# A recommendation tower on one core: group transposes issued two groups of products ahead, and two small layers as three fp32r calls

## The reference

```python
e = jnp.stack([tbl_0[ids[:, 0]], ..., tbl_26[ids[:, 26]]], axis=1)     # (2048, 27, 128)
interactions = jnp.einsum('bfd,bgd->bfg', e, e)
flat_interactions = interactions[:, _TRIU_I, _TRIU_J]                  # 351 a sample
h = jnp.concatenate([e.reshape(B, -1), flat_interactions, dense_ctx], axis=1)
h = jnp.maximum(h @ W_top1 + b_top1, 0.0)      # (3823, 512)
h = jnp.maximum(h @ W_top2 + b_top2, 0.0)      # (512, 256)
y = h @ W_top3                                 # (256, 1)
```

## Time and profile before

| | us |
|---|---|
| median of 3 runs | 712.8 |
| lowest and highest of them | 710.17 and 718.01 |
| the profiled execution | 709.83 |
| its span | 708.0 |
| TensorE busy, share of the span | 574.9, 81% |
| GpSimd busy, share of the span | 416.2, 59% |
| mean granted clock of TensorE | 0.908 |

### The profile page before, as it was taken

One profiled execution on the slowest core, in us unless ns is written; L12 is line 12 of the kernel. 1 busy time (PEld: TensorE's weight loads), 2 busy tenths in 40 slices (PEclk: granted clock), 3 DMA queues, 4 the chain that ended last, 5 costly groups with the idle time before them and its releaser, 6 DMA issues.

```text
span 708.0 us, 7882 instructions
## 1 busy us (share of the span) xinstructions
PE 574.9 (81%) x2578; PEld 504.6 (71%) x2578; DVE 347.6 (49%) x1140; ACT 232.3 (33%) x703; POOL 416.2 (59%) x450
## 2 busy tenths in 40 slices
PE   2606688989889898959959896897968979698898
PEld 1505577868778787948848795786857868697786
DVE  4305462819264563808337281554707355372755
ACT  4204423324251513315232331514315161323441
POOL 6775565666666565665746667365664666556001
PEclk9956899989989998989989899799987999989999
DMA  6613411111111111111111111011110111111000
GB/s 211 217 52 110 131 45 44 46 46 44 45 45 50 41 49 41 48 45 39 47 29 50 44 42 52 27 49 42 46 52 26 49 41 49 42 41 46 12 1 1
DMA packets 19581, 37.84 MB, mean 53 GB/s; under 512 B 7780, under 2 KB 8804, under 8 KB 19540
## 3 DMA queue, kind: packets, MB, share of 16 engines
q0 software_dynamic: 13824, 28.34, 15.1%
q1 hardware_dynamic: 5716, 8.99, 4.0%
HBM read 37.30 MB, written 0.01 MB: 53 GB/s over the span
## 4 chain that ended last, share of the span: by engine, by line
PE 59%; another core or an unknown queue 20%; DVE 8%; issue 6%; ACT 5%; DMA 1%; SPq 0%; ACTq 0%; DVEq 0%
PE ps_acc L298 12%; PE ps_acc L299 11%; PE ps_acc L300 11%; PE ps_gram L323 10%; DVE g_buf L666 6%; PE ps_acc L356 6%; PE ps_t L269 5%; PE ps_gram L400 3%; ACT g_buf L582 2%; DVE emb_x L645 1%; DMA g_buf<-in_W_top 1%; ACT emb_x L534 1%; ACT h_t L571 1%; PE ps_gram L352 1%
## 5 line engine op out<-in xcount | busy, mean ns | idle before, releaser
L242 POOL DMA_INDIRECT emb<-in_tbl,idx x405 | 385.8, 953 | 233.4 <-issue 109.4
L298 PE MATMUL ps_acc<-w_hi,emb_x 128*128 128x512 f32 x432 | 211.1, 489 | 28.7 <-DVE emb_x L645 26.6
L645 DVE TENSOR_TENSOR emb_x<-ps_t,emb_x 128x512 fp32r<-128x512 f32 (+1 forms) x111 | 73.9, 667 | 249.6 <-ACT emb_x L534 165.2
L299 PE MATMUL ps_acc<-w_lo,emb_x 128*128 128x512 f32 x432 | 182.7, 423 | 0.0
L300 PE MATMUL ps_acc<-w_hi,emb_x 128*128 128x512 f32 x432 | 181.0, 419 | 0.0
L666 DVE COPY g_buf<-ps_gram 32x112 f32<-32x112 f32 x480 | 129.8, 270 | 93.6 <-PE ps_gram L323 63.1
L323 PE MATMUL ps_gram<-emb_x 128*128 128x224 f32 x480 | 99.5, 335 | 79.2 <-DVE emb_x L645 41.2
L298 PEld LDWEIGHTS ps_acc<-w_hi,emb_x 128*128 128x128 f32 x432 | 131.9, 305 | 35.3 <-DVE emb_x L645 28.0
L323 PEld LDWEIGHTS ps_gram<-emb_x 128*128 128x128 f32 x480 | 83.4, 231 | 102.0 <-DVE emb_x L645 45.1
L582 ACT ACTIVATE g_buf<-ps_gram 32x112 f32<-32x112 f32 x480 | 122.2, 255 | 99.0 <-PE ps_gram L323 64.8
L534 ACT ACTIVATE emb_x<-ps_t 128x512 fp32r<-128x512 f32 (+1 forms) x111 | 63.1, 583 | 272.7 <-PE ps_t L269 137.4
(11 more groups left out here) (61 smaller groups left out, 163.2 us busy)
## 6 DMA issues: line engine op xcount, KB each, us to landing
g_buf<-in_W_top SPq DMA_DIRECT2D x27, 256.0 KB
emb<-in_tbl,idx POOLq DMA_INDIRECT x405
w_cols<-in_W_top SPq DMA_DIRECT2D x1, 512.0 KB
w<-in_W_top SPq DMA_DIRECT2D x1, 512.0 KB
emb<-in_tbl,idx_first POOLq DMA_INDIRECT x27
w_cols<-in_W_top SPq DMA_DIRECT2D x1, 222.0 KB
idx<-in_ids SPq DMA_DIRECT2D x1, 216.0 KB, 4.9
ctx_rows<-in_dense_ctx SPq DMA_DIRECT2D x4, 32.0 KB
```

The source lines that it names most:

```text
L242: pool.indirect_dma_start(out=emb[:, f * D:(f + 1) * D], out_offset=None, in_=tables[f], in_offset=bass.IndirectOffsetOnAxis(ap=rows, axis ...
L298: pe.matmul(acc, emb_part(0, f), w_hi[:, f, :], start=(f == 0), stop=False)
L299: pe.matmul(acc, emb_part(0, f), w_lo[:, f, :], start=False, stop=False)
L645: dve.tensor_tensor(group_part(1, g), turned_bank(n, g), group_part(0, g).bitcast(fp32), ALU.subtract).then_inc(s_emb_lo, 1)
```

## The change

Three things are changed.

First, the order on TensorE from the second tile on. The turn of a group now stands two groups of features ahead of the features that use it, and the last group is turned before the columns are multiplied. The order of a tile becomes: turn 2, features 0 to 3, turn 3, features 4 to 7, turn 4, features 8 to 11, turn columns, turn 5, features 12 and 13, turn 6, multiply columns, features 14 to 17, turn h1, gram stage with five features in it as before, layer 2, features 23 to 26. ScalarE and VectorE follow: `take_columns` moves behind the split of group 4, and `relu_h1` and `take_h1` behind the split of the last group.

Second, the columns and layer 2 get high and low parts as layer 1 has. Each fp32 call becomes three fp32r calls. ScalarE's copies write the high parts as before; VectorE gets new instructions for the low ones (`split_columns`, two of them a tile, and `split_h1`, one).

Third, the weights of those two layers are split too, in the second tile. They are loaded into places that are free then (the upper part of `g_buf`, `gram`, `h1`), in six transfers where there were four, after all layer-1 weights are split, and cost ScalarE and VectorE five instructions each, once.

The last tile keeps its own order, with the same replacement of calls.

```diff
             def multiply_columns(t):
-                pe.wait_ge(s_cols_out, t + 1)
+                pe.wait_ge(s_cols_hi, t + 1)
                 if t == 0:
-                    pe.wait_ge(s_w_late, 64)
+                    pe.wait_ge(s_late_lo, NCC)
                 for n in range(NCC):
-                    last = multiply_chunk(t, n)
+                    multiply_chunk_hi(t, n)
+                pe.wait_ge(s_cols_lo, t + 1)
+                for n in range(NCC):
+                    last = multiply_chunk_lo(t, n)
                 last.then_inc(s_acc, 1)
...
+            def layer_2(t, acc):
+                pe.wait_ge(s_h1_hi, t + 1)
+                pe.wait_ge(s_h1_lo, t + 1)
+                if t == 0:
+                    pe.wait_ge(s_late_lo, len(LATE))
                 for k in range(K2):
-                    last = pe.matmul(ps_late[:, 0:H2], h1_t[:, k * P:(k + 1) * P], w_2[:, k, :],
-                                     start=(k == 0), stop=(k == K2 - 1))
-                last.then_inc(s_l2, 1)
...
-            BEFORE_UNIT = [2, 0, 0, 2, 0, 0, 1, 0, 0, 1, 0, 0, 1, 0, 0, 0]
-            assert len(BEFORE_UNIT) == UNITS and sum(BEFORE_UNIT) <= NF - 4 * GF
+            BEFORE_UNIT = [0, 0, 0, 2, 0, 0, 1, 0, 0, 1, 0, 0, 1, 0, 0, 0]
...
             for t in range(TILES - 1):
...
+                else:
+
+
+                    turn_group(t, 2)
+                    multiply_next(GF)
+                    turn_group(t, 3)
+                    multiply_next(GF)
+                    turn_group(t, 4)
+                    multiply_next(GF)
                     turn_columns(t - 1)
-                turn_group(t, 4)
-                if t > 0:
+                    turn_group(t, 5)
+                    multiply_next(2)
+                    turn_group(t, 6)
                     multiply_columns(t - 1)
-                multiply_group(t, 3)
-                turn_group(t, 5)
-                if t > 0:
+                    multiply_next(4)
                     turn_h1(t - 1)
...
                 if t > 0:
-                    layer_2(t - 1)
-                while f < NF:
-                    multiply(t, f)
-                    f += 1
+                    layer_2(t - 1, ps_late[:, 0:H2])
+                multiply_next(len(todo))
...
             for t in range(TILES - 1):
                 for g in range(NG):
...
-                    if t > 0 and g == 3:
+                    if t == 1:
+                        for c in LATE_AT[g]:
+                            split_late_weights(c)
+                    if t > 0 and g == 4:
                         take_columns(t - 1)
-                    if t > 0 and g == 4:
+                    if t > 0 and g == 6:
                         relu_h1(t - 1)
-                    if t > 0 and g == 5:
                         take_h1(t - 1)
...
+            def split_columns(t):
+                dve.wait_ge(s_cols_hi, t + 1)
+                dve.tensor_tensor(cols_lo[:, 0:FULL * P], ps_late[:, 0:FULL * P],
+                                  cols_hi[:, 0:FULL * P].bitcast(fp32), ALU.subtract)
...
+            def split_h1(t):
+                dve.wait_ge(s_h1_hi, t + 1)
+                dve.tensor_tensor(h1_lo[:, :], ps_late[:, :], h1_hi[:, :].bitcast(fp32),
+                                  ALU.subtract).then_inc(s_h1_lo, 1)
...
+                        if g == 4:
+                            split_columns(t - 1)
+                        if g == 6:
+                            split_h1(t - 1)
```

More of the change, by code:

```diff
@@ L138, in dlrm_tower_kernel @@
         s_stored = sem("s_stored")
+        LATE = []
+        for n in range(NCC):
+            k = P if n < FULL else REST
+            place = g_buf[0:k, (STAGES - 2 + n) * H1:(STAGES - 1 + n) * H1]
+            LATE.append((place, w_cols_hi[0:k, n, :], w_cols_lo[0:k, n, :]))
+        gram_words = gram[:, :, :].rearrange("p f g -> p (f g)")
+        LATE_AT = [[0, 1, 2], [3], [4], [], [], [], []]
+        for k, place in ((0, gram_words[:, 0:H1]), (2, h1[:, :])):
+            LATE.append((place, w_2_hi[:, k:k + 2, :].rearrange("p k n -> p (k n)"),
+                         w_2_lo[:, k:k + 2, :].rearrange("p k n -> p (k n)")))
         def emb_part(part, f):
@@ L769, in _ @@
             pack_pairs(t, 0, POOL_FROM)
+            for n in range(NCC):
+                split_last_chunk(t, n)
             layer_3(t - 1)
-            take_left_h1(t)
+            split_last_h1(t)
             last_layer_3(t)
```

185 lines of the change are left out of this document (124 added, 61 removed).

## The result

The changed kernel takes 774.9 us (median of 4 runs, 770.9 to 786.3) against 714.1 us for the kernel before beside it. The ratio is 1.083, with a 95% interval from 1.073 to 1.094: slower, where 656 us had been forecast. Its span is 784.2 us, and the mean granted clock fell from 0.908 to 0.869.

What follows compares the result with a forecast made beforehand. It took TensorE to set the pace, waiting on late signals. 14 tiles from 41.2 to 37 us save 58.8 us, once-costs add 2 us: span 651 us; plus 1.8 and 3 us: 656 us, range 610 to 704 us.

Steps and rivals of the forecast that it cites:

- What bounds the kernel: Ahead of the gram stage TensorE idles 6.10 us in the shown tile, mostly for its last turn's late signal.
- The order: Between last turn and gram stage, 5.5 us of work instead of 1.4 us hides 4.3 of 6.5 us lateness.
- fp32 to fp32r: Columns 2.28 to 2.15 us, layer 2 1.54 to 1.45 us; together about 0.2 us a tile saved.
- The floor of 34 us from GpSimd: 27 gathers at 0.95 us plus 0.30 us between two, without pause, allow no tile under 34 us.
- The failed step: At the turn of h1 ahead of the gram stage, 3 us of lateness a tile remain, between nothing and 6.1 us.
- Slower: two late signals in a row: Rival: columns' and turn of h1's signals both 6.5 us late; 43.8 us a tile, 751 us; chance 0.09.
- a sign of being wrong: Any signal lateness above 6.5 us in the new order would show the forecast wrong.
- moves with the work: Rival: turn of h1 signals 6.5 us late, the fourth gram unit waits 6.1 us; 693 us; chance 0.20.
- Floor: Rival: late signals go with the old order, GpSimd sets 34 us a tile; 614 us; chance 0.13.
- TensorE really busy: Rival: TensorE executes in the gap ahead of the gram stage; only 0.2 us a tile saved; 712 us; chance 0.08.
- The rule that was weighed: Matmul ends are computed, so TensorE may execute in apparent idle time; the sum would be only 0.2 us a tile.
- one rival only: The rival of 34 us a tile set by GpSimd, 614 us, chance 0.13; the first tile's 27 us piece spoke against it.

Runs made afterwards that it cites:

- new_order_no_gathers: The changed kernel, gathering only for the first tile, with all later tiles computing on the first tile's rows: 557.9 us, 32.4 us a tile.
- calls_only: The kernel before in its old order, with the new fp32r calls, splits and late weights: 717.0 us, ratio 1.0035.
- gate_columns: The changed kernel, with GpSimd waiting for TensorE's columns signal ahead of group 5: 584.2 us (before: 581.7) in the second session, 710.6 us (before: 710.2) in the third.
- after_again: The changed kernel, unchanged, run again in the third session: 773.8 us, ratio 1.092 to the kernel before; its trace is of 775.4 us.
- before_again: The kernel before, unchanged, run again for a trace in the third session: traced run 706.6 us, where the kernel before took 710.2 us.
- order_only: The kernel before with the new order on all engines and the old fp32 calls: 760.5 and 772.5 us, 1.071 and 1.088 times the kernel before.
- space_large: The changed kernel with three one-column memsets by GpSimd after each gather: 696.5 us, ratio 0.980 to the kernel before.
- no_gathers: The kernel before, gathering only for the first tile, with all later tiles computing on the first tile's rows: 583.9 us, 33.5 us a tile.

## Why the prediction was wrong

**What bounds the kernel: right, as far as it went.** The late signal of TensorE ahead of the gram stage was the wait to look at the earlier trace rows. Without it and its like a tile takes 33.5 us instead of 40.2 us. What I left open, "Why it is late, the trace doesn't tell", decided everything.

**The order: the arithmetic held.** With prompt signals the new order takes 32.4 us a tile (new_order_no_gathers), against a forecast of 33.2 us if TensorE waited for nothing. The turn of h1 with its four features of cover cost nothing there.

**fp32 to fp32r: right.** Nine column calls take 2.21 us (153.83 to 156.04 us after), 2.15 us forecast. Layer 2 takes some 1.4 us (315.03 to 316.31 us and one call more, in new_order_no_gathers), 1.45 us forecast. calls_only: no difference.

**The floor of 34 us from GpSimd: right.** 34.0 us a tile in gate_columns with prompt signals.

**The failed step: "I take 3 us a tile, between them, because signals were prompt at 432.51 us and 6.5 us late 9 us later in one and the same tile."** I treated the lateness as a fixed amount that belongs to a place, of which the new order would cover 4.3 us, and I bounded what is left by what the old order shows, 6.1 us. Measured, TensorE's idle time ahead of the turn of h1 and of the gram units together is 9.8 us a tile (8.4 us in after_again), where the old order has 5.3 us.

The lateness is neither fixed nor tied to a place. It goes with how long gathers have followed one another 1.25 us apart. In the old order GpSimd catches up with TensorE and stops for lack of a turned group: in 14 tiles the columns end 9.1 to 10.5 us after its last stop (a pause over 0.8 us), and their signal is at most 1.5 us late (2.3 us in before_again). The new order turns the groups earlier, so that GpSimd has work laid out past the columns: in the first tile shown above it issues gathers without a stop from 144.54 us to 164.35 us and, after 0.47 us, to 168.26 us. In eleven tiles the columns now end 11.6 us or more after its last stop, and their signal is 4.3 to 15.5 us late; in the two tiles where they end some 3 us after a stop, and in the last one, with no gathers left, it is prompt. It isn't a rule without exceptions: one tile is 9.1 us late 0.6 us after a stop, and two tiles of order_only are under 0.8 us late 12 us after one. (GpSimd's idle time for turns is longer after, 139.7 against 94.0 us, but it comes in fewer stops, 36 over 0.8 us from 60 us on against 43.) The relu and the turn of h1 stand behind the columns' signal, and the tile went from 40.2 us up to 45.1 us. That the stream of gathers is the cause, and not the order by itself, is shown by new_order_no_gathers (prompt, faster than the old order's 33.5 us a tile), by gate_columns in the third session (one stop more, 63 us back) and by space_large (another rate, all signals prompt).

**The rivals.** "Slower: two late signals in a row" was the one: the place, the relu's wait, and the sign. I gave it 751 us and a chance of 0.09; it came out at 775, and with a lateness far above the 6.5 us that I had named as a sign of being wrong. "Against it: nothing in the shown tile is late right behind the columns" was true of the whole old order, where that signal is at most 2.3 us late in every tile of both traces; it said nothing of an order in which the columns come later in a stream of gathers. The lateness "moves with the work" was also partly seen: 54.9 us are left ahead of gram units, 35.2 of them on ScalarE's takes. "Floor" is what a chip with prompt signals gives. "TensorE really busy": refuted, since without gathers the same matmuls run 33.5 us a tile.

**The rule that was weighed.** The Trainium skill (Perfetto Trace Analysis, Per-engine timelines) says that a matmul's end in a profile is computed. The runs agree that the modelled end isn't when the others learn of it, up to 15.5 us apart here; but where signals are prompt the next engine starts 0.03 to 0.1 us behind it, and no work was hidden in the gap: without gathers the same matmuls take 33.5 us a tile.

**What could have been read.** The earlier trace rows has GpSimd's idle time by what ended it, 94.0 us of it on turns: these stops were the thing to count. And the first tile's unknown piece of 27 us, from 28.19 us, ends 3.1 us after a run of gathers that goes on without a pause until 52.56 us in GpSimd's timeline; I used it as evidence against one rival only.

**What stays open.** Why TensorE's signals wait for a stream of gathers is not settled. Those of ScalarE and VectorE don't where it can be read: in the trace of the changed kernel VectorE's 28 waits for ScalarE's copies of the columns and of h1 end within 0.03 us, and TensorE's waits for the relu and for takes of the gram stage within 0.06 us. The number of gathers (or of their rows) counts, not the bytes, and a rate between one in 1.36 and one in 1.52 us is the limit. A queue that TensorE's signals share with the gathers would behave so, but no run shows it, and the 23 late signals that were seen in mid-stream are not explained. Nor is it shown what makes one chip, or session, of five prompt.

## What to carry to other kernels

A late signal is a cost with a cause of its own: before an order is built around it, find what else is running when it is late, and how long it has been, over several tiles and not one; and take it away in one run, as no_gathers did here. A reordering that keeps an engine off the critical path evenly fed also takes away its pauses, and here TensorE's signals had lived on them. Where indirect gathers run back to back beside TensorE, try fewer or more widely spaced ones, or plain transfers, and time the result on more than one chip.

## What the runs showed of the hardware

- While GpSimd issues indirect gathers 1.25 us apart, other engines see TensorE's signals up to 15.5 us after the modelled end; 37 of 60 late ones were seen while GpSimd stood still. At 1.52 us apart no wait of ScalarE or VectorE for TensorE ended over 0.1 us late. Beside the late signals, the waits for ScalarE and VectorE named above ended within 0.06 us.
- 27 plain transfers of 64 KB a tile, as large as the gathers and released by the same turns, leave the signals prompt (33.5 us a tile, against 40.0).
- The kernel before took 709.8, 581.7, 710.2, 710.3 and 693.6 us on five chips, one session on each, a spread of 22%.
- On one chip, going from one idle memset after each gather to three made a kernel 8.5% faster (761.1 to 696.5 us); on another, two made the kernel before 6.7% slower.
- GpSimd takes one small memset in the 0.30 us between two gathers for nothing.
